# An LSTM on one core: the gate sums of a step in two PSUM banks of half width, and the gate chain on all 128 features at once

## The reference

```python
xW = jnp.einsum('ntd,dg->ntg', x, Wx) + b
c0 = jnp.zeros_like(h0)
def step(carry, xw_t):
    prev_h, prev_c = carry
    a = xw_t + prev_h @ Wh
    i = jax.nn.sigmoid(a[:, :Hd])
    f = jax.nn.sigmoid(a[:, Hd:2 * Hd])
    o = jax.nn.sigmoid(a[:, 2 * Hd:3 * Hd])
    g = jnp.tanh(a[:, 3 * Hd:])
    next_c = f * prev_c + i * g
    next_h = o * jnp.tanh(next_c)
    return ((next_h, next_c), next_h)
```

## Time and profile before

| | |
|---|---|
| median of 3 runs | 2726.16 us (2726.15 to 2726.85) |
| profiled execution | 2726.29 us |
| its span, first to last instruction | 2724.5 us |
| instructions | 121148 |
| PE busy | 2671.2 us, 98%, 49152 matmuls |
| PEld busy | 1387.0 us, 51%, 49152 loads |
| DVE busy | 1929.8 us, 71% |
| ACT busy | 1245.7 us, 46% |
| mean granted TensorE clock | 0.989 |
| DMA | 109.94 MB, 40 GB/s |

### The profile page before, as it was taken

The page is one execution under the profiler, slowest core; times in us unless marked ns, Lnnn a source line. Parts: engine busy times, 40 slices in busy tenths (PEclk is TensorE's granted clock), DMA queues, the critical chain, the costliest instruction groups (busy, mean ns, idle before and its releaser), DMA issues.

```text
span 2724.5 us, 121148 instructions
## 1 busy us (share of the span) xinstructions
PE 2671.2 (98%) x49152; PEld 1387.0 (51%) x49152; DVE 1929.8 (71%) x8121; ACT 1245.7 (46%) x3722; POOL 45.9 (2%) x134
## 2 busy tenths in 40 slices
PE   3999999999999999999999999999999999999998
PEld 0455555555555555555555555555555555555554
DVE  6777777777777777777777777777777777777776
ACT  3444444444444444444444444444444444444444
POOL 0000000000000000000000000000000000000000
PEclk6999999999999999999999999999999999999999
DMA  6111111111111111111111111111111111111111
GB/s 144 37 43 35 38 38 40 35 39 42 35 38 38 40 35 39 42 35 38 38 39 35 39 42 35 39 38 39 35 39 42 35 39 39 38 35 39 42 36 26
DMA packets 223520, 109.94 MB, mean 40 GB/s; under 512 B 25216, under 2 KB 222464, under 8 KB 222464
## 3 DMA queue, kind: packets, MB, share of 16 engines
q1 hardware_dynamic: 223488, 109.48, 15.7%
HBM read 75.83 MB, written 33.55 MB: 40 GB/s over the span
## 4 chain that ended last, share of the span: by engine, by line
PE 97%; issue 1%; DVE 1%; DMA 1%; SPq 0%; ACT 0%; POOL 0%; DVEq 0%; POOLq 0%
PE Z L244 97%; DMA wx_raw<-in_Wx 1%; DVE wh_lo L435 0%; SPq L213 0%; SPq L200 0%; DVE wmax L417 0%; SPq L208 0%; DVE h_hi L475 0%; ACT tanh_c L356 0%; POOL wmax_all L537 0%; DVE xmax L396 0%; DVE x_lo L381 0%; DVE zs L407 0%; DVE c L490 0%; DVE scales L410 0%
## 5 line engine op out<-in xcount | busy, mean ns | idle before, releaser
L350 ACT ACTIVATE act<-Z,scales 128x192 f32<-128x192 f32 x1022 | 430.9, 422 | 1159.5 <-PE Z L244 1159.5
L244 PE MATMUL Z<-wx_hi,x_hi 128*32 128x512 f16 x8176 | 807.7, 379 | 9.3 <-DVE x_lo L381 9.3
L244 PE MATMUL Z<-wh_hi,hT_hi 128*32 128x512 f16 x8176 | 808.1, 379 | 8.0 <-DVE hT_hi L480 8.0
L244 PE MATMUL Z<-wh_lo,hT_hi 128*32 128x512 f16 x8176 | 808.1, 379 | 0.0
L244 PE MATMUL Z<-wx_hi,x_lo 128*32 128x512 f16 x8176 | 807.6, 379 | 0.0
L244 PE MATMUL Z<-wx_lo,x_hi 128*32 128x512 f16 x8176 | 807.6, 379 | 0.0
L244 PE MATMUL Z<-wh_hi,hT_lo 128*32 128x512 f16 x8176 | 533.1, 379 | 0.0
L486 DVE TENSOR_TENSOR fc<-act,c 128x64 f32<-128x64 f32 x512 | 115.3, 225 | 570.2 <-ACT act L350 570.2
L356 ACT ACTIVATE tanh_c<-c 128x64 f32<-128x64 f32 x1024 | 262.3, 256 | 269.7 <-DVE c L497 249.2
L475 DVE SCALAR_TENSOR_TENSOR h_hi<-act,scales,tanh_c 128x64 f16<-128x64 f32 x1024 | 291.3, 285 | 113.1 <-ACT tanh_c L356 86.3
L327 ACT ACTIVATE Z<-bias_bc,scales 128x512 f32<-128x512 f32 x511 | 344.6, 674 | 0.0
(11 more groups left out here) (50 smaller groups left out, 1286.1 us busy)
## 6 DMA issues: line engine op xcount, KB each, us to landing
x_in<-in_x SPq DMA_DIRECT2D x512, 64.0 KB, 2.0
x_res<-in_x SPq DMA_DIRECT2D x512, 64.0 KB, 2.1
out_y<-y SPq DMA_DIRECT2D x512, 64.0 KB, 1.7
wx_raw<-in_Wx SPq DMA_DIRECT2D x16, 256.0 KB, 8.8
wh_raw<-in_Wh SPq DMA_DIRECT2D x16, 256.0 KB, 19.0
bias_bc<-in_bias SPq DMA_DIRECT2D x4, 64.0 KB, 2.0
h_in<-in_h SPq DMA_DIRECT2D x4, 16.0 KB, 13.8
```

The costliest lines, as they stand in the source:

```text
L244: return nc.tensor.matmul(bank[L * j:L * j + B, :], lhsT, rhs, start=False, stop=last, skip_group_check=True)
L350: nc.scalar.activation(half_gates(act, a)[:, 0:3], half_gates(Z[s], a)[:, 0:3], ACT.Sigmoid, scale=scale).then_inc(sig_done, 1)
```

## The change

A step's Z now lies in two banks: columns of i and f (a = 0) in one, of o and g (a = 1) in the other, 256 columns each (HW). Two pairs of banks serve the four steps in turn: steps s and s + 2 share a pair, each with its own half of the columns. Every matmul is cut in two of 256 columns, one for each bank, with a weight load each; a group becomes two half groups. In the last part of a step, with `hT_lo`, all chunks of a = 0 come before those of a = 1, so that the sums of i and f end four half groups ahead of the others, and `z_done` is signalled twice. PE waits for `hT_hi` once, as a whole. ACT takes sigmoid of i and f at the first signal, tanh of g and then sigmoid of o at the second. DVE and ACT work on all 128 features at once in the rest of the chain. The bias is placed in both banks with one instruction, after the sigmoid of o four steps back.

```diff
+        Z = [bank_pair(f"Z{q}") for q in range(2)]
...
+        def z_half(s, a):
+            return Z[s % 2][:, a, s // 2 * HW:(s // 2 + 1) * HW]
...
+        def columns(w, ch, j, a):
+            return w[:, ch, j * ZW + a * HW:j * ZW + (a + 1) * HW]
...
                 for ch in range(NCH):
                     for xp, wp in ((x_hi, wx_hi), (x_hi, wx_lo), (x_lo, wx_hi)):
+                        for a in range(2):
+                            for j in range(NJ):
+                                mm = add(s, a, j, xp[:, r, ch, s * B:(s + 1) * B], columns(wp, ch, j, a))
+                mm.then_inc(xpart_done, 1)
+
+            def recurrent_part(t, s):
+                pe.wait_ge(hT_hi_done, t)
+                for ch in range(NCH):
+                    for w in (wh_hi, wh_lo):
+                        for a in range(2):
+                            for j in range(NJ):
+                                add(s, a, j, hT_hi[:, ch, :], columns(w, ch, j, a))
+                pe.wait_ge(hT_lo_done, t)
+
+                for a in range(2):
+                    for ch in range(NCH):
                         for j in range(NJ):
-                            mm = add(Z[s], j, xp[:, r, ch, s * B:(s + 1) * B], wp[:, ch, j * ZW:(j + 1) * ZW])
-                mm.then_inc(xpart_done, 1)
-
-            def recurrent_part(t, s):
-                for part, ht in enumerate((hT_hi, hT_lo)):
-                    for ch in range(NCH):
-                        if part == 0 and ch % 2 == 0:
-                            pe.wait_ge(hT_hi_done, 2 * t - 1 + ch // 2)
...
+                            mm = add(s, a, j, hT_lo[:, ch, :], columns(wh_hi, ch, j, a), ch == NCH - 1)
+                    mm.then_inc(z_done, 1)
...
+                at = s // 2 * HW
+                nc.scalar.activation(Z[s % 2][:, :, at:at + HW], bias_bc[:, :].rearrange("p (a w) -> p a w", a=2),
+                                     ACT.Copy, scale=scale).then_inc(bias_placed, 1)
...
+                    sc.wait_ge(z_done, 2 * t + 1)
+                    nc.scalar.activation(act[:, 0:2 * C], z_half(s, 0), ACT.Sigmoid, scale=scale).then_inc(sig_done, 1)
+                    sc.wait_ge(z_done, 2 * t + 2)
+                    nc.scalar.activation(act[:, 3 * C:], z_gate(s, 3), ACT.Tanh, scale=scale).then_inc(tanh_g_done, 1)
+                    nc.scalar.activation(act[:, 2 * C:3 * C], z_gate(s, 2), ACT.Sigmoid, scale=scale).then_inc(sig_o_done, 1)
+                    sc.wait_ge(c_done, t + 1)
+                    nc.scalar.activation(tanh_c[:, :], c[:, :], ACT.Tanh).then_inc(tanh_c_done, 1)
...
+                v.wait_ge(sig_done, t + 1)
+                nc.vector.tensor_tensor(fc[:, :], act[:, C:2 * C], c[:, :], ALU.mult)
+                v.wait_ge(tanh_g_done, t + 1)
+                nc.vector.tensor_tensor(ig[:, :], act[:, 0:C], act[:, 3 * C:], ALU.mult).then_inc(ig_done, 1)
+                v.wait_ge(ig_done, t + 1)
+                nc.vector.tensor_tensor(c[:, :], fc[:, :], ig[:, :], ALU.add).then_inc(c_done, 1)
+                v.wait_ge(sig_o_done, t + 1)
+                v.wait_ge(tanh_c_done, t + 1)
+                nc.vector.scalar_tensor_tensor(h_hi[:, :], act[:, 2 * C:3 * C], h_scale(q), tanh_c[:, :],
+                                               ALU.mult, ALU.mult).then_inc(h_hi_done, 1)
+                v.wait_ge(h_hi_done, t + 1)
+                nc.vector.transpose(hT_hi[:, :, :], h_hi[:, :].rearrange("p (ch l) -> p ch l", ch=NCH)).then_inc(hT_hi_done, 1)
```

More of the change, by code:

```diff
@@ L39, in sb, with bank_pair @@
             return ctx.enter_context(nc.sbuf_tensor(name, shape, dt))
-        def bank(name):
-            return ctx.enter_context(nc.psum_tensor(name, [P, 512], F32))
+        def bank_pair(name):
+            return ctx.enter_context(nc.psum_tensor(name, [P, 2, 512], F32))
         def sem(name):
@@ L93, in lstm_residual @@
         scales = sb("scales", [P, 2, 4], I32)
-        Z = [bank(f"Z{s}") for s in range(TB)]
+        Z = [bank_pair(f"Z{q}") for q in range(2)]
         wx_loaded = [sem(f"wx_loaded{ch}") for ch in range(NCH)]
@@ L135, in lstm_residual @@
         tanh_g_done = sem("tanh_g_done")
+        sig_o_done = sem("sig_o_done")
         ig_done = sem("ig_done")
@@ L151, in lstm_residual, with z_gate @@
         h0_view = h0.rearrange("b (j c) -> j b c", j=NJ)
[L153 to L159, removed]
+        HW = ZW // 2
+        def z_half(s, a):
+            return Z[s % 2][:, a, s // 2 * HW:(s // 2 + 1) * HW]
+        def z_gate(s, g):
+            at = s // 2 * HW + g % 2 * C
+            return Z[s % 2][:, g // 2, at:at + C]
+        def columns(w, ch, j, a):
+            return w[:, ch, j * ZW + a * HW:j * ZW + (a + 1) * HW]
         def by_tile(w):
@@ L220, in _ @@
             sp.wait_ge(x_turned, 1)
-            sp.wait_ge(banks_opened, TB)
+            sp.wait_ge(banks_opened, 4)
             load_x(2, 0)
@@ L241, in _, with add @@
         def _(pe):
-            def add(bank, j, lhsT, rhs, last=False):
-                return nc.tensor.matmul(bank[L * j:L * j + B, :], lhsT, rhs, start=False, stop=last, skip_group_check=True)
+            def add(s, a, j, lhsT, rhs, last=False):
+                return nc.tensor.matmul(z_half(s, a)[L * j:L * j + B], lhsT, rhs, start=False, stop=last, skip_group_check=True)
             pe.wait_ge(x_turned, 1)
[L248 to L252, removed]
+            for q in range(2):
+                for a in range(2):
+                    for j in range(NJ):
+                        mm = nc.tensor.matmul(Z[q][L * j:L * j + B, a], x_T[:, 0, 0, :],
+                                              x_in[:, 0].rearrange("p t c -> p (t c)"), start=True, stop=True)
+                    mm.then_inc(banks_opened, 1)
             pe.wait_ge(bias_placed, 1)
@@ L257, in _ @@
                 pe.wait_ge(wx_loaded[ch], 16 * NJ)
-                raw = by_tile(wx_raw[:, ch])
-                for j in range(NJ):
-                    add(Z[0], j, x_T[:, ch, 0, :], raw[:, j])
+                for a in range(2):
+                    for j in range(NJ):
+                        add(0, a, j, x_T[:, ch, 0, :], by_tile(wx_raw[:, ch])[:, j, 2 * a:2 * a + 2])
             pe.wait_ge(h0_turned, 1)
@@ L263, in _ @@
                 pe.wait_ge(wh_loaded[ch], 16 * NJ)
[L264 to L267, removed]
+                for a in range(2):
+                    for j in range(NJ):
+                        mm = add(0, a, j, h0_T[:, ch, :], by_tile(wh_raw[:, ch])[:, j, 2 * a:2 * a + 2], ch == NCH - 1)
+                    if ch == NCH - 1:
+                        mm.then_inc(z_done, 1)
             def input_part(t, s, r):
@@ L325, in place_bias @@
                 if started(t - TB):
-                    sc.wait_ge(tanh_g_done, 2 * (t - TB) + 2)
-                nc.scalar.activation(Z[s][:, :], bias_bc[:, :], ACT.Copy, scale=scale).then_inc(bias_placed, 1)
+                    sc.wait_ge(sig_o_done, t - TB + 1)
+                at = s // 2 * HW
+                nc.scalar.activation(Z[s % 2][:, :, at:at + HW], bias_bc[:, :].rearrange("p (a w) -> p a w", a=2),
+                                     ACT.Copy, scale=scale).then_inc(bias_placed, 1)
             sc.wait_ge(bias_loaded, 16 * NJ)
-            sc.wait_ge(banks_opened, TB)
+            sc.wait_ge(banks_opened, 4)
             place_bias(0, 0, 1.0)
@@ L471, in prepare @@
                     cut_w_lo(1, ch)
[L473 to L481, removed]
@@ L483, in step @@
             def step(t, s, r):
                 q = r if s < TB - 1 else 1 - r
[L485 to L497, removed]
@@ L498, in step @@
-                turn_high_part(t, 0)
-                high_part_of_h(t, 1, q)
-                turn_high_part(t, 1)
+                v.wait_ge(sig_done, t + 1)
[4 more added lines that the diff above has]
+                nc.vector.tensor_tensor(c[:, :], fc[:, :], ig[:, :], ALU.add).then_inc(c_done, 1)
```

## The result

The changed kernel takes 3360.86 us (median of four, 3353.77 to 3372.37); the one before 2726.38. The ratio is 1.233, 95% interval 1.229 to 1.237: slower by 634 us, where 183 were forecast. The forecast (2909, range 2750 to 3040) had the direction and what turned out to be the cause, and far too low a price.

What follows compares the result with a forecast made beforehand. The prediction took PE, busy 98% of the span, as the bound. It summed 2726.3 + 30.2 (matmuls) + 153 (code fetched at jumps) - 0.9 (shorter chain at the end) = 2909 us, range 2750 to 3040.

Steps and rivals of the forecast that it cites:

- The bound: Whole span: PE, busy 98%, sets the time; a shorter chain from sums to hT_hi gives nothing.
- The chain: Gates to hT_hi on 128 features: still fits beside PE's matmuls, some 0.25 us to spare, so costs nothing.
- A: The start of ScalarE's first operation on a step's sums, from which the chain's times are counted.
- The matmuls: PE's half groups: the fixed 2.5 ns of each group is paid twice, +30.2 us.
- the code kept: Rival: PE's longer loop body stays in its code store and is not fetched again; 2756 us, chance 0.15.
- paced loads: Rival: weight loads pace PE's half groups at 115 ns; 3054 us, or 2901 with code kept; chance 0.06.
- the 2.5 ns by columns: Rival: PE's extra 2.5 ns goes by columns, not instructions, and the code stays; 2725 us, chance 0.04.
- a gain by alternating banks: Rival: the 2.5 ns are turnaround in one bank and alternating drops them; 31 us less, 2695, chance 0.03.
- The code: PE's loop body grows from 6 pages to 12, is not kept, and is fetched at every jump; chance 0.62.
- Price of a jump: PE's 60 jumps back: each waits 2F - 1.65 = 2.55 us for two pages, +153 us.
- F: Time from asking for a page of code to running it: taken as 2.1 us, bounds 1.1 and 3.2.
- The clock: Rival: code is fetched and PE's clock falls after each jump's idle stretch; +130, about 3039 us, chance 0.10.

Runs made afterwards that it cites:

- the kernel with the short loop: The changed kernel with PE's loop one block long (four steps, 1536 instructions), high and low parts of x in one buffer, cut one step later: 2760.24 us.
- the moved head: The changed kernel with PE's loop head put on the first instruction of a page of code: 3278.09 us.
- the half-width kernel on one bank: The kernel before with only the matmuls cut in two of 256 columns, both into the same bank, chain in halves as before: 3329.64 us.
- 8 groups cut: The kernel before with 8 of a step's 24 matmul groups cut in halves, same bank: 2988.30 us.
- 3 groups cut: The kernel before with 3 of a step's 24 matmul groups cut in halves: 2926.73 us, or 2730.62 with the loop head on a page.
- `BODY = 4`: The kernel before with four blocks written out in the loop body in place of two, 28 jumps back for 60: 2823.08 us.

## Why the prediction was wrong

**The bound: right.** PE sets the time, the chain's length gives nothing, and the losses are all PE's.

**The chain: right in its sum.** Forecast A + 2.45 ready and A + 2.74 needed. In the kernel with the short loop:

```profile
1005.31 0.47 ACT L370 ACTIVATE act<-Z,scales 128x256 f32<-128x256 f32 x1 [2.86 <-PE Z L257]
...
1007.60 0.31 DVE L505 STREAM_TRANSPOSE hT_hi<-h_hi 128x128 f16<-128x128 f16 x1
...
1008.03 0.22 PEld L257 LDWEIGHTS Z<-wh_hi,hT_hi 128*32 128x32 f16 x8
```

Ready at A + 2.60, loaded at A + 2.72. It fits with 0.1 us, not 0.25: VectorE's operations on 128 elements of act took 0.29 us, not the 0.25 of h in the earlier trace rows. The chain alone on one bank, 117 us slower, shows what the lead of the four half groups is for.

**The matmuls: right.** Forecast 109.2 ns and 2756 us with the code kept; measured 109.2 and 2760.24, 34 us above before for the 29.3 forecast. The fixed 2.5 ns belong to the instruction. The rivals of paced loads, of the 2.5 ns by columns and of a gain by alternating banks fall with this kernel. The Trainium skill's rule of pairs (TensorE: Matmul & The Clock Gate, "Back-to-back issue gap"), taken as the prediction tried it, as 25 ns on each half group, does not hold for four narrow loads side by side: 109.2 ns are 256 columns and the 2.5 ns.

**The code: right in kind.** The body of 12.1 pages touches 13 and is fetched in every pass, 887 packets for some 750 forecast. The Trainium skill (Advanced Engine Details and Errata, "ISA Cache") gives TensorE 128 KB in lines of 16 KB, which are eight; that agrees with the seven touched pages plus one of the table above. The "Only 2 cache lines!" of the same section does not fit TensorE here: a body touching seven pages moved no code.

**Price of a jump: the step that failed**, in three places.

1. *F was taken at 2.1 us.* The two gaps are 3.06 + 2.03 = 5.1 us in the pass shown and 3.03 + 2.29 = 5.3 us in the mean of all 60, for 2.55 forecast. With the 0.25 of cover the first gives F = 3.3, just above even the upper bound of 3.2 (one landing and one packet). The head left only 54 instructions in its page (0.74 us), not the 103 (1.4 us) that the prediction counted; with them the second gives F = 3.0. So in this kernel the form of the term holds to 0.3 us, and F was too small: 319 us for 153. The form does not carry over as it is: the first gap is 3.6 us with the moved head and 4.4 in the half-width kernel on one bank, and why is open.
2. *The clock.* "Against it: that idle stretch was 8 us". This rival had 0.10. A gap of 3 us was enough: in 29 of the 60 passes the clock fell before the second gap began, in the other 31 within it. Of the lowered 6.8 us of the pass shown, 2.04 are its own cost; over all passes that cost is 133 us. The lower level took 390 us more than before over the span, 6.5 a jump, but for some 120 of these PE stood in its gaps anyway.
3. *"Pages in line are asked for 3.5 us ahead and are no wait."* With F near 3.3 and a page that lasts 256 x 13.65 ns = 3.5 us it is a race, and PE lost it at some 295 page ends in this trace. They cost 127 us, and 19 more lie in smaller delays that were not placed, 146 in all. With matmuls of 512 columns, whose pages last twice as long, no page in line was late. Whether the time of a packet or its latency decides the race was not tested.

So, in the profiled execution (3356.4 us, 630 above before): 34 (matmuls) + 319 (gaps of the jump) + 133 (clock) + 146 (pages in line) = 632, 2 too many. The three terms of the code come from the starts of all matmuls against a steady 109.2 ns, and their sum, 598, agrees with the 600.6 that the kernel with the short loop gave back (this execution is 4.5 us below the median). The forecast's own range ended at 3041 because F was bounded by DMA rows (x_res still lands in 2.2 us), and because the clock and the pages in line, 279 us together, stood in it at nothing.

**Left open.** Why the first page ends behind a jump are in time and the later ones not. Why the first gap of a jump differs from kernel to kernel, 2.2 to 4.4 us. And what decides, beside a gap's length, whether the clock falls: it fell at all 60 jumps of the changed kernel, at 26 of 60 with 8 groups cut, and at only 9 of 60 with 3 groups cut, where the one gap of a jump is 2.5 to 3.2 us.

## What to carry to other kernels

Count the instructions of a loop's body on each engine before cutting instructions finer, above all on PE where every matmul brings a load: here seven touched pages of 256 instructions are free and the eighth costs 200 us in 60 passes. The queue of code packets in the profile tells which side one is on; a body near the edge can be saved by the place of its head alone. And an engine that is busy for all of the span can be made slower by more instructions for the same total work, although its waits name no other engine.

## What the runs showed of the hardware

- A jump to code that is no longer there left PE idle for 2.88 us (matmuls 3.06 us late), and the page behind it for 1.79 more; with matmuls twice as long (512 columns) the matmuls came 2.1 and 1.2 us late.
- Two kernels alike but for the loop head's place in its page differ by 196 us (2730.62 and 2926.73).
- The queue moved 9 pages of code in every pass of a loop that touches eight, 10 for nine, 14 for the thirteen of the changed kernel, and none for seven.
- At ends of pages in line, 126 to 128 half-width matmuls apart, PE was late some 295 times (127 us in all); with 512 columns, never (50 waits in the `BODY = 4` kernel, all right behind its jumps).
- The granted clock fell to 0.50 for 6.8 us after PE had stood 3.06 us between stretches of full work. Gaps of 2.5 to 3.2 us let it fall at 9 of 60 jumps in one kernel (3 groups cut).
- PEld at 97% busy went with no loss: 95234 loads in 2600 us, four side by side.
